# Layers 1 to 3 of a four-layer stack written out for the four sequences, and a layer's first input fetched by the layer before

## The reference, cut to what matters

```python
x = L0_attn_x                                   # (4, 1024, 256)
x = _layernorm(x + _L0_attn_ref(x, ...))        # layer 1: gated linear attention, causal
x = _layernorm(x + _L0_ffn_ref(x, ...))         # layer 2: attention, 8 heads, values and outputs by expert
x = _layernorm(x + _L1_attn_ref(x, ...))        # layer 3: attention, 16 heads, keys gated by a small network
x = _layernorm(x + _L1_ffn_ref(x, ...))         # layer 4: feed-forward network, 256-1024-1024-1024-256
```

## Time and profile before

| | |
|---|---|
| median of 3 runs | 3596.03 us (3595.15 to 3611.57) |
| the profiled execution | 3602.37 us |
| its span in the trace | 3600.7 us, 50745 instructions |
| TensorE busy | 3239.3 us, 90% of the span |
| VectorE, ScalarE, GpSimd busy | 1953.9, 1509.1, 842.4 us |
| mean granted clock of TensorE | 0.955 of full speed |
| layer 1's loop | 18.7 to 309.5 us, 216 matmuls in a pass |
| layer 2's loop | 356.2 to 2004.0 us, some 1960 matmuls in a pass |
| layer 3's loop | 2029.8 to 2897.5 us |

### The profile page before, as it was taken

The page is one execution under the profiler, slowest core; times in us unless marked ns, Lnnn a source line. Parts: engine busy times, 40 slices in busy tenths (PEclk is TensorE's granted clock), DMA queues, the critical chain, the costliest instruction groups (busy, mean ns, idle before and its releaser), DMA issues. The chain is left out here.

```text
span 3600.7 us, 50745 instructions
## 1 busy us (share of the span) xinstructions
PE 3239.3 (90%) x18306; PEld 2331.5 (65%) x18306; DVE 1953.9 (54%) x3377; ACT 1509.1 (42%) x2795; POOL 842.4 (23%) x753
## 2 busy tenths in 40 slices
PE   7895999889988999889989698998989979999998
PEld 4554755876568755777558554646556468888887
DVE  4344843867458654677439374765747533333332
ACT  2331144422444134431544455474655634444443
POOL 1121511653037411554027300101000011111111
PEclk9897999999999999999999899999999989999999
DMA  5111100210021100211012101000010030000000
GB/s 190 47 35 66 30 19 13 91 43 24 10 59 49 48 15 16 83 46 30 10 43 64 48 2 26 1 2 25 2 25 2 14 160 12 13 18 12 7 6 12
DMA packets 189927, 127.33 MB, mean 35 GB/s; under 512 B 125808, under 2 KB 174192, under 8 KB 186224
## 3 DMA queue, kind: packets, MB, share of 16 engines
q1 hardware_dynamic: 189680, 124.02, 12.2%
HBM read 106.52 MB, written 28.44 MB: 37 GB/s over the span
## 5 line engine op out<-in xcount | busy, mean ns | idle before, releaser
L1610 ACT ACTIVATE l3b_prob<-sums 128x512 f32<-128x512 f32 (+3 forms) x768 | 332.9, 494 | 207.3 <-PE sums L1543 168.3
L648 POOL TENSOR_TENSOR l_qrow<-l_vm,l_qst 128x512 fp32r<-128x512 f32 x256 | 364.0, 1435 | 205.8 <-ACT l_qst L642 187.0
L1859 PE MATMUL sums<-l_uhi,l_h 128*128 128x512 f32 x1024 | 409.1, 399 | 0.0
L1859 PE MATMUL sums<-l_ulo,l_h 128*128 128x512 f32 x1024 | 403.1, 394 | 0.0
L976 DVE TENSOR_REDUCE l2b_mx<-sums 128x1 fp32r<-128x1024 f32 (+7 forms) x256 | 192.6, 758 | 301.1 <-PE sums L888 299.4
L944 ACT ACTIVATE sb_nx<-sums 128x512 f32<-128x512 f32 (+3 forms) x384 | 181.9, 492 | 355.8 <-PE sums L905 351.2
L913 PE MATMUL sums<-sb_nx,l_vx 128*128 128x512 f32 (+3 forms) x768 | 302.4, 503 | 13.0 <-ACT l_od L951 13.0
L1538 PE MATMUL sums<-l_qst,l_kst 64*128 64x512 f32 (+3 forms) x768 | 276.3, 426 | 21.5 <-DMA l_qst<-l3b_peak 10.9
L1945 DVE TENSOR_TENSOR l_ulo<-l_made,l_uhi 128x512 fp32r<-128x512 f32 x128 | 90.5, 707 | 362.1 <-ACT l_uhi L1876 362.0
L642 ACT CAST l_qst<-l_vm 128x512 fp32r<-128x512 f32 x256 | 157.4, 619 | 240.0 <-DVE l_vm L635 239.6
L1521 PE MATMUL sums<-l_kst,l_qst 64*128 64x512 f32 (+3 forms) x768 | 237.6, 431 | 20.6 <-DVE l3b_low L1622 11.4
(11 more groups left out here) (270 smaller groups left out, 7870.8 us busy)
## 6 DMA issues: line engine op xcount, KB each, us to landing
l_ve<-ve SPq DMA_DIRECT2D x34, 512.0 KB, 4.1
l_oe<-oe SPq DMA_DIRECT2D x16, 1024.0 KB, 6.3
l_vm<-weights_copy SPq DMA_DIRECT2D x64, 176.0 KB, 2.3
sb_nx<-between SPq DMA_DIRECT2D x9, 1024.0 KB, 5.6
weights_copy<-h SPq DMA_DIRECT2D x2, 4096.0 KB, 26.6
l_ve<-inverse SPq DMA_DIRECT2D x32, 256.0 KB, 3.6
l_qst<-l3b_peak SPq DMA_DIRECT2D x512, 0.5 KB, 2.0
l_h<-weights_copy SPq DMA_DIRECT2D x2, 4096.0 KB, 23.6
```

The costliest lines, as they stand in the source:

```text
L648: pool.tensor_tensor(rlo[:, i % RT, :], routed[:, i % RT, :], rhi[:, i % RT, :].bitcast(F32), ALU.subtract).then_inc(s3.routed_lo, 1)
L1610: act.activation(prob[:, i % RB, j, a, 0:hi - lo], bank(m.ps, part % SCORE, 0, hi - lo), ACT.Exp, scale=SCALE1).then_inc(s.exp_ready, 1)
L1859: run(lambda out, a, x, first, last: pe.matmul(out, a, x, start=first, stop=last))
```

## The change

The three `Fori` loops become Python loops, so that the four passes stand one after the other in each engine's program, with constant addresses. Tiles that a pass allocates get `b` in their names. Layer 1's last pass fetches `dst[0]`, which is layer 2's first input, in place of the tokens of sequence 0. Layer 2's `fetch_first` gets no source, and TensorE's turns no longer wait for its normalized tiles. Lines behind L588 move up by one.

```diff
@@ -296,7 +296,7 @@
-    with nc.Fori(0, SEQS) as b:
+    for b in range(SEQS):
@@ -437,7 +437,7 @@
             def _(sp):
-                fetch_load(sp, m, s, src[(b + 1) % SEQS])
+                fetch_load(sp, m, s, src[b + 1] if b + 1 < SEQS else dst[0])
                 store(sp, s, y, dst[b])
@@ -585,7 +585,6 @@
     def by_tensor(pe):
         for t in range(NT):
-            pe.wait_ge(s0.nx_ready, t + 1)
             entry_turn(pe, t)
         pe.wait_ge(ld.weights, 16 * 7)
         gate_logits(pe)
@@ -616,7 +615,7 @@
-    fetch_first(nc, m, s0, src[0], load, by_tensor=by_tensor, by_vector=by_vector, by_scalar=by_scalar, by_pool=by_pool)
+    fetch_first(nc, m, s0, None, load, by_tensor=by_tensor, by_vector=by_vector, by_scalar=by_scalar, by_pool=by_pool)
@@ -809,7 +808,7 @@
-        sb = lambda name, shape, dt=F32: own.enter_context(nc.sbuf_tensor("l2b_" + name, shape, dt))
+        sb = lambda name, shape, dt=F32: own.enter_context(nc.sbuf_tensor(f"l2b_{name}_{b}", shape, dt))
...
@@ -1710,11 +1709,11 @@
-    with nc.Fori(0, SEQS) as b:
+    for b in range(SEQS):
         with ExitStack() as own:
-            projections(own)
+            projections(own, b)
```

More of the change, by code:

```diff
@@ L1004, in output_experts @@
     def output_experts(own, b):
-        sb = lambda name, shape, dt=F32: own.enter_context(nc.sbuf_tensor("l2c_" + name, shape, dt))
+        sb = lambda name, shape, dt=F32: own.enter_context(nc.sbuf_tensor(f"l2c_{name}_{b}", shape, dt))
         ohi1 = krow[:, 0:2, :].rearrange("p a (e d) -> p (a e) d", d=D)
@@ L1260, in layer3, with projections @@
         fetch_first(nc, m, s0, None, load, by_scalar=by_scalar, by_pool=by_pool)
-    def projections(own):
-        sb = lambda name, shape, dt=F32: own.enter_context(nc.sbuf_tensor("l3a_" + name, shape, dt))
+    def projections(own, b):
+        sb = lambda name, shape, dt=F32: own.enter_context(nc.sbuf_tensor(f"l3a_{name}_{b}", shape, dt))
         xT = sb("xT", [P, KC, T])
@@ L1445, in attention @@
     def attention(own, oraw, b):
-        sb = lambda name, shape, dt=F32: own.enter_context(nc.sbuf_tensor("l3b_" + name, shape, dt))
+        sb = lambda name, shape, dt=F32: own.enter_context(nc.sbuf_tensor(f"l3b_{name}_{b}", shape, dt))
         s = s2
@@ L1636, in output @@
     def output(own, oraw, b):
-        sb = lambda name, shape, dt=F32: own.enter_context(nc.sbuf_tensor("l3c_" + name, shape, dt))
+        sb = lambda name, shape, dt=F32: own.enter_context(nc.sbuf_tensor(f"l3c_{name}_{b}", shape, dt))
         y = sb("y", [P, NT, D])
@@ L1711, in _ @@
                 store(sp, s, y, dst[b])
-    with nc.Fori(0, SEQS) as b:
+    for b in range(SEQS):
         with ExitStack() as own:
-            projections(own)
+            projections(own, b)
         with ExitStack() as own:
-            oraw = own.enter_context(nc.sbuf_tensor("l3_oraw", [P, GROUPS, T], F32))
+            oraw = own.enter_context(nc.sbuf_tensor(f"l3_oraw_{b}", [P, GROUPS, T], F32))
             with ExitStack() as inner:
```

## The result

| | before | changed |
|---|---|---|
| median | 3599.55 us | 3553.61 us |
| the profiled execution | 3602.37 us | 3555.41 us |
| its span in the trace | 3600.7 us | 3553.7 us |
| mean granted clock | 0.955 | 0.961 |

What follows compares the result with a forecast made beforehand. TensorE bounds the kernel, idling at loop back edges and at layer 2's entry. Branches 24.1, entry 12.9 and clock 3.0 sum to 40.0 us off the profiled 3602.4, or 3556.0 us from the median 3596.0; range 3542 to 3574.

Steps and rivals of the forecast that it cites:

- The branches: Taken branches at loop ends go: 12.2 us in layer 2, 11.2 in layer 3, 0.7 in layer 1, sum 24.1.
- Rival 1: Any jump out of a long pass waits, written out or not: only 13.6 us gained, 3582.4 us; chance 0.10.
- rival 2: Code passed only once is fetched at each block entry: 57 us slower, 3653 us; chance 0.03.
- The 0.2 us behind the barrier: At each of the nine pass boundaries, TensorE's first product was to start this long behind the barrier.
- Layer 1: Its three short taken branches at the loop end go: 3 x 0.22 = 0.7 us.
- The entry: Where layer 2 begins: its first load, statistics and normalization leave the path, gate's products start earlier, 12.9 us gained.
- the estimate of 321 to 321.6: Time in us by which layer 2's last weight load lands at its entry, just ahead of the turns' end.
- the lower bound of 11.1: Gain in us at layer 2's entry if the weights land no faster than before.
- The tables: Layer 3 loads one activation table fewer in its first pass, two fewer in each later one: zero gain.
- The clock: Six restarts at 1.2 GHz in layers 2 and 3 shorten from 4.45 to 3.4 us each: 3 us gained.
- clock stays up: No fall at all six later-pass boundaries of layers 2 and 3: 50 us gained in all, 3546 us; chance 0.10.
- third rival: Clock at six boundaries decides more: up at all, 3546 us, chance 0.10; long restart at each, 3563 us, chance 0.05.

Runs made afterwards that it cites:

- experiment 1: Against the kernel before: layers 1, 2, 3 written out singly, 3593.81, 3595.59, 3591.47 us; two passes per loop body in layers 1 and 2, 3596.77 us.
- Experiment 2: Changed kernel with the old entry into layer 2 (its weight block loads and normalizes its own first input): 3575.94 us beside 3609.4 of the kernel before.
- Experiment 7: Changed kernel with an Exp ahead of layer 3's entry copies, two more table loads a pass: its first blocks took 47.8, 47.7, 48.4 and 49.6 us.
- e6_tables: Changed kernel with a 128-element Exp before ScalarE's copies in layer 3, two more table loads a pass; only block times given, 47.7 to 49.6 us.
- e7_other_way: Changed kernel with layer 4's branch turned round, the products that run straight behind it: 3552.33 us, ratio 0.9840 to the kernel before.
- experiment 3: Changed kernel rerun unedited, 3562.67 us, and with 64 or 32 useless TensorE products ahead of everything to move code pages, whose total times are not given.
- r1_changed_again: The changed kernel once more without an edit, on another chip: 3562.67 us beside 3609.64 of the kernel before, ratio 0.9867.
- experiment 5: Changed kernel with useless products filling TensorE's idle time at the pass ends of layers 2 and 3: 3554.58 us, 8.1 less than the changed kernel.
- e2_layer2: The kernel before with layer 2 alone written out: 3595.59 us beside 3609.4, ratio 0.9961.
- e8_warm: Changed kernel with 10 useless TensorE products ending each layer 2 pass and 12 each layer 3 pass: 3554.58 us, 8.1 less than the changed kernel.

## Why the prediction was right, point by point

**The branches: right.** Six waits of 23.4 us were to go, and they went, each with its own loop, one price per taken branch (experiment 1). Rival 1 would have kept them all; rival 2 would have put new ones at the block entries, and there is none: TensorE waits 12.7 us in all at the start of layer 2's third blocks, before and after. The 0.2 us behind the barrier was 0.3 in layer 2 and 0.1 in layer 3.

**Layer 1: mis-sized.** The term was 0.7 us, the three short branches. Layer 1 got 2.8 us shorter. Looped, its later first blocks take 37.2 to 37.6 us and once in each of three traces 38.7 or 38.8, with 12.8 to 13.1 us at the low clock; written out 36.7 to 37.4. So some 0.5 us a pass, and one clock event of over 1 us. The branch row gives the branch alone, 0.2 us. Behind the barrier stand the counter and the gaps around both as well: TensorE starts layer 1's third pass 0.5 us behind the barrier looped and 0.1 us written out. Before and changed:

```profile
164.97 4.12 PE L220 MATMUL sums<-sb_ident,sb_nx 128*128 128x128 f32 x16 [4.05 <-PEq L383]
162.18 4.09 PE L220 MATMUL sums<-sb_ident,sb_nx 128*128 128x128 f32 x16 [3.49 <-PEq L383]
```

The second blocks, 35.1 us looped and 34.9 written out, give another 0.6 us in four passes; no term held them. I had looked at the branch rows and not at the blocks behind them.

**The entry: right.** 12.9 forecast; 13.6 with what stands between the layers, 13.4 for the block alone. Experiment 2 gives 12.5 to 13.5 by the medians and 11.4 by its trace, where VectorE's long tile held up no turn. The prediction had put the 11.3 us of the turns down to that long tile rightly; that it was a matter of timing and worth 1.6 us, it didn't say. The turns step by 1.15 us and not 1.21, which is where 0.5 us lies: the 1.21 had been read off the last step of the old form. The weights landed by 317.9, 8.7 us behind the block's start; the estimate of 321 to 321.6 is 8.4 to 9.0 us behind the block's start in the kernel before, 312.6. So they came as estimated, 0.7 us ahead of the products, and the lower bound of 11.1 was not reached.

**The tables: about right.** Zero was forecast. Experiment 7 gives 0 to 0.9 us a pass for two loads more.

**The clock: right in kind, low in size.** The low stretches are 3.4 us, as read from the earlier trace rows. What the shorter restarts are worth is the length of the first blocks less their branches: 100.5, 100.5, 99.3 before and 99.4, 99.2, 99.3 after in layer 2, 2.4 us, and likewise 2.6 us in layer 3. That is some 5 us where 3.0 stood. The term took the middle of two restarts, 4.45 us from TensorE's return to full clock; the six took 5.8, 5.9, 3.2, 6.0, 3.4 and 4.8 us, 4.9 in the mean. With 3.4 after the change that gives 4.3 us, and some 0.6 us is left over, in layer 3, where the table loads went too. Of the idle time, "2.7 to 3.3 us" was 2.5 and 3.1. The case "clock stays up" of the third rival didn't come in the profiled execution, but it isn't ruled out: without any filling the clock stayed up at 10 of 48 such boundaries (experiment 5), never at all six of one execution.

**What was in no term.** Layer 2's third blocks lost 4.8 us. A second execution of the kernel lost 4.9, but the same code in `e6_tables` and `e7_other_way` had the long block of pass 3 alone of the two; a code page that meets a load has a part in it (experiment 3). Against it, layer 3's weight block (1.4 us), its first pass (1.4; its first block was at the lower clock for 2.9 us instead of 5.7) and its other blocks (4.7) were shorter. The 4.7 are clock scatter: the same blocks of `r1_changed_again` took 666.8 us, more than before. So the 7 us by which the sum fell short of the profiled 47.0 are made of terms that were too small, 2.1 (layer 1), 0.7 (entry) and 2.0 (clock and tables), and of 2.2 us net of things that no term held and that another execution has otherwise.

## What to carry to other kernels

Read the loop lines' branch rows and not only the engines' waits: a hardware loop whose body is 1604 matmuls or more pays some 4 us at each taken branch, one of up to 432 some 0.2 us (some 0.5 us with counter and gaps), so write out the long ones first. A forward jump pays as well, 6.0 us at layer 4's `If`: put the case that runs straight behind the branch, and the far jump where something covers it. And where a stage's first load can be issued in the stage before, its whole chain of load, statistics and normalization leaves the path.

## What the runs showed of the hardware that was not expected

- A jump can be paid twice: 6.0 to 7.0 us in front of layer 4, and 3.4 and 3.8 us more five products later in two kernels (`e2_layer2`, `e8_warm`). That these are the ones where it landed near a page's end is inferred from the length of the code ahead.
- The fetch of a 16 KB page of TensorE's code, one packet on one queue, can delay 1 MB loads that are under way by 1.0 to 1.4 us, though not each time, and it moves when code far ahead of it changes length. The Trainium skill (Runtime: NRT & Kernel Launch, Instruction fetch mechanics) calls crossing a page mostly hidden; of TensorE itself that is so here (151 pages in the changed kernel, and no wait for "issue" over 0.6 us but layer 4's), of the loads beside it not quite.
- Filling 2 us of standing still at a barrier with products without use kept the clock up at 12 of 12 boundaries. Without filling it fell at 38 of 48, and each fall cost 1.5 to 1.7 us.
- One tile of VectorE's normalization took 3.7 us and not 0.4 while GpSimd's cast of 3.6 us ran; it cost 1.6 us or nothing, by which of the eight tiles it was.
